# Binarised convolutions and a spline: mask rows interleaved by channel, the step chain on GpSimd, one load moved ahead of one store

## What is computed

```
out = relu(batchnorm(conv3x3(x, sign(w1))))       # gamma1, beta1; mean and variance over images and pixels
out = batchnorm(conv3x3(out, sign(w2)))           # gamma2, beta2
x   = relu(out + x)

u = (clip(x * a + b, -1.5, 1.5) + 1) * 0.5 * 31   # per channel a, b
i = floor(u);  t = u - i                          # cubic B-spline with 32 knots
spline = sum over n of alpha_table[clip(i + n - 1, 0, 31)] * basis_n(t)     # n = 0..3, 8 values each
y = id_gain * x + sum over r of spline[r] * mix[channel, r] + bias
```

## Time and profile before

| | us |
|---|---|
| median of 3 runs | 1140.85 |
| lowest, highest | 1138.58, 1143.94 |
| the profiled execution, as timed | 1139.08 |
| its span, from the first to the last instruction | 1137.2 |
| PE busy in it | 1081.0 (95%) |
| DVE busy | 966.2 (85%) |
| ACT busy | 899.3 (79%) |
| POOL busy | 137.5 (12%) |

### The profile page before, as it was taken

The page is one execution under the profiler, slowest core; times in us unless marked ns, Lnnn a source line. Parts: engine busy times, 40 slices in busy tenths (PEclk is TensorE's granted clock), DMA queues, the critical chain, the costliest instruction groups (busy, mean ns, idle before and its releaser), DMA issues.

```text
span 1137.2 us, 53175 instructions
## 1 busy us (share of the span) xinstructions
PE 1081.0 (95%) x24650; PEld 724.2 (64%) x24650; DVE 966.2 (85%) x959; ACT 899.3 (79%) x410; POOL 137.5 (12%) x195
## 2 busy tenths in 40 slices
PE   6999999699999968999999999999999999999996
PEld 5777777577777745556656656656666556656564
DVE  5856656687767779999999999999999998999997
ACT  4445443767777648999999999999999999999971
POOL 6000000058100000101101011011110110101100
PEclk9999999899999989999999999999999999999999
DMA  8677674677677936799898989989989988998652
GB/s 288 221 293 285 251 278 175 224 248 298 263 284 291 349 164 161 185 233 225 228 234 213 237 203 234 222 220 235 228 209 235 226 225 212 233 233 200 165 131 87
DMA packets 57465, 259.46 MB, mean 228 GB/s; under 512 B 16080, under 2 KB 16080, under 8 KB 49232
## 3 DMA queue, kind: packets, MB, share of 16 engines
q1 hardware_dynamic: 48496, 208.40, 54.6%
q0 software_dynamic: 8640, 48.17, 23.2%
q10 hardware_dynamic: 160, 0.30, 0.1%
HBM read 104.29 MB, written 77.07 MB: 159 GB/s over the span
## 4 chain that ended last, share of the span: by engine, by line
PE 86%; DVE 7%; issue 3%; DMA 1%; ACT 1%; SPq 0%; DVEq 0%; ACTq 0%
PE tab L1303 49%; PE acc L741 30%; PE tab L1313 7%; DVE middle_mask L1161 1%; DMA halo<-y_scratch 1%; DVE far_sq L1210 1%; DMA w_raw<-in_w 1%; ACT xin L381 1%; ACT yout L420 1%; DVE poly L1202 0%; DVE far L1188 0%; DVE stats L547 0%; DVE offset L1154 0%; DVE poly L1216 0%; DVE band_split L509 0%
## 5 line engine op out<-in xcount | busy, mean ns | idle before, releaser
L1303 PE MATMUL tab<-edge_mask,diag 128*32 128x392 bf16 x10240 | 446.6, 329 | 5.8 <-issue 2.5
L1303 PEld LDWEIGHTS tab<-edge_mask,diag 128*32 128x32 f16 x10240 | 283.5, 97 | 160.6 <-issue 20.1
L1058 ACT ACTIVATE edge_mask<-cell,thr 128x6272 bf16<-128x6272 bf16 x62 | 338.6, 5509 | 2.0 <-DMA cell<-cell 2.0
L420 ACT ACTIVATE yout<-acc 128x1568 f32<-128x1568 f32 x64 | 94.5, 1477 | 167.5 <-PE acc L741 146.9
L741 PE MATMUL acc<-band_split,w 64*64 64x385 f16 (+2 forms) x4608 | 194.6, 329 | 9.9 <-DVE band_split L509 4.9
L741 PE MATMUL acc<-split,w 64*64 64x385 f16 (+3 forms) x4608 | 191.5, 326 | 11.2 <-DVE w L468 10.0
L1303 PE MATMUL tab<-middle_mask,diag 128*32 128x392 bf16 x4096 | 187.2, 329 | 7.5 <-issue 5.5
L547 DVE BATCH_NORM_STATS2 stats<-yout 128x392 f32 (+1 forms) x240 | 117.9, 555 | 89.1 <-ACT yout L420 89.1
L741 PEld LDWEIGHTS acc<-band_split,w 64*64 64x64 f16 x4608 | 150.0, 109 | 54.3 <-issue 8.8
L741 PEld LDWEIGHTS acc<-split,w 64*64 64x64 f16 x4608 | 144.7, 108 | 57.1 <-issue 11.9
L1303 PEld LDWEIGHTS tab<-middle_mask,diag 128*32 128x32 f16 x4096 | 110.6, 97 | 72.6 <-DVE middle_mask L1161 10.4
(11 more groups left out here) (140 smaller groups left out, 962.0 us busy)
## 6 DMA issues: line engine op xcount, KB each, us to landing
y_scratch<-yout SPq DMA_DIRECT2D x32, 1568.0 KB, 6.2
cell<-cell SPq DMA_DIRECT2D x496, 98.0 KB, 4.6
xin<-y_scratch SPq DMA_DIRECT2D x16, 1568.0 KB, 6.2
lin<-far POOLq DMA_DIRECT2D x32, 784.0 KB, 8.6
out<-lin SPq DMA_DIRECT2D x31, 784.0 KB, 5.3
xin<-in_x SPq DMA_DIRECT2D x15, 1568.0 KB, 6.5
lin<-y_scratch SPq DMA_DIRECT2D x30, 784.0 KB, 9.3
lin<-in_x POOLq DMA_DIRECT2D x28, 784.0 KB, 7.9
```

Source lines behind the costliest of these rows:

```text
L420: act.activation(yout[b][:, :].rearrange("p (r k x) -> p k r x", r=2, k=TILES)[:, 2 * part:2 * part + 2], acc[:, 4 * part:4 * part + 4, 0: ...
L1058: act.activation(mask_of(c, q)[:, :, :], cell4[c % 2][:, :, :], ACT.Sign, bias=thr[:, q:q + 1]).then_inc(sign_mask_ready, 1)
L1303: mm = pe.matmul(tab[(c + t) % 2][j * GROUP:(j + 1) * GROUP, sub, 0:SUB], keep["diag"][part][:, j % 2, t, q, :], mask_of(c, q)[:, j, sub * ...
```

## The change

- **Mask rows.** Channel k of a block now stands on rows 4 k + g instead of 32 g + k. The 16 copies of a chunk write every fourth partition, `cell4[g:P:4]`, where they wrote 32 partitions in a row. `ident4`, `thr`, `above` and `mix_by_group` follow this order. GpSimd makes them with selects, a fold and 12 small arithmetic instructions instead of 32 memsets. `mix_by_group` is no longer loaded by 8 small DMAs but copied by 8 GpSimd instructions from `mix_sb`. `spread_cells` uses one matmul with 128 columns of weights where it used four with 32. Its weights lie in `dist_sq`, which for that is allocated for the whole kernel.
- **The steps' chain** moves from DVE to GpSimd, where it can run as soon as the coefficients are there, in the first convolution. With the new row order it takes 42 instructions. The last five instructions of `coefficients` no longer wait for each other.
- **SP's order.** At the end of the first convolution the load of pair 17 is issued before the store of pair 15, not after it.

The diff, cut to its core:

```diff
@@ -236,9 +241,6 @@
-                for g in range(4):
-                    sp.dma_start(mix_by_group[:, half, g * GROUP:(g + 1) * GROUP],
-                                 mix_t[:, half * GROUP:(half + 1) * GROUP]).then_inc(small_loaded, 16)
@@ -292,8 +294,8 @@
                         sp.wait_ge(stored[b], 16)
                         for to, frm in load(PAIRS + b, b, 1):
                             sp.dma_start(to, frm).then_inc(loaded[b], 16)
-                    if b == 0 and is_last(n):
-                        store(2 * i + 1, 1)
+                if is_last(n):
+                    store(2 * i + 1, 1)
@@ -309,6 +311,40 @@
+            def fold(t, width):
+                while width > 1:
+                    width //= 2
+                    link(pool.tensor_tensor(t[:, 0:width], t[:, 0:width], t[:, width:2 * width], ALU.add))
+            def steps():
+                for l in range(3):
+                    link(pool.tensor_tensor(step[:, l, :, :], coef[:, l, :, 1:CENTRES], coef[:, l, :, 0:STEPS],
+                                            ALU.subtract))
...
+                for half in range(2):
+                    for odd, quads in enumerate((EDGE_QUADS, MIDDLE_QUADS)):
+                        to = dsel[:, half, :, quads[0]:quads[1] + 1]
+                        for g in range(4):
+                            frm = step[:, 1 + half, :, 2 * g + odd:STEPS:8]
+                            if g == 0:
+                                link(pool.tensor_scalar(to, frm, of_group[:, g:g + 1], None, ALU.mult))
+                            else:
+                                link(pool.tensor_scalar(own_step[:, :, :], frm, of_group[:, g:g + 1], None, ALU.mult))
+                                link(pool.tensor_tensor(to, to, own_step[:, :, :], ALU.add))
...
@@ -319,19 +355,34 @@
+            link(pool.memset(keep["spread"][:, :, :], 0.0))
+            link(pool.affine_select(out=keep["spread"][:, :, :], in_=keep["spread"][:, :, :], compare_op=ALU.not_equal,
+                                    fill=1.0, base=0, pattern=[[-1, P], [0, 4]], channel_multiplier=1))
...
-                                        base=-g * GROUP, pattern=[[-1, GROUP]], channel_multiplier=1))
+                                        base=-g, pattern=[[-4, GROUP]], channel_multiplier=1))
...
+            pool.wait_ge(small_loaded, 5 * 16)
+            for half in range(2):
                 for g in range(4):
...
+                    pool.tensor_copy(mix_by_group[:, half, g:P:4],
+                                     mix_sb[:, half * GROUP:(half + 1) * GROUP]).then_inc(mix_spread, 1)
...
-            pool.wait_ge(steps_ready, 1)
+            pool.wait_ge(coefficients_ready, TABLES)
+            steps()
@@ -688,8 +719,6 @@
                     take_stats(2 * i, 0, base)
-                    if n == half_rounds:
-                        steps()
@@ -714,7 +743,8 @@
-                pe.wait_ge(small_loaded, 13 * 16)
+                pe.wait_ge(small_loaded, 5 * 16)
+                pe.wait_ge(mix_spread, 8)
@@ -935,7 +965,7 @@
-                        sp.dma_start(cell4[c % 2][g * GROUP:(g + 1) * GROUP, j, :],
+                        sp.dma_start(cell4[c % 2][g:P:4, j, :],
                                      cell[c % 2][j * GROUP:(j + 1) * GROUP, :]).then_inc(copied[c % 2], 16)
@@ -1320,13 +1350,11 @@
-                        for g in range(4):
-                            mm = pe.matmul(tab[s][g * GROUP:(g + 1) * GROUP, 2 * (j % 2) + u, 0:SUB],
-                                           ones[:, 2 * GROUP * j + 1:2 * GROUP * (j + 1):2],
-                                           cell[0][:, (2 * h + u) * SUB:(2 * h + u + 1) * SUB], start=True, stop=True)
+                        mm = pe.matmul(tab[s][:, 2 * (j % 2) + u, 0:SUB],
+                                       keep["spread"][:, j * GROUP:(j + 1) * GROUP, :],
+                                       cell[0][:, (2 * h + u) * SUB:(2 * h + u + 1) * SUB], start=True, stop=True)
```

68 lines of the change are left out of this document (38 added, 30 removed).

## The result

The changed kernel takes **1128.09 us** (median of 5, 1126.97 to 1131.77). The kernel before takes 1139.11 us (median of 5: the three runs that the prediction started from, and two more). The ratio is 0.990 [0.9874, 0.9925], so the gain is 11.0 us where 6.0 were forecast. The profiled execution took 1127.08 us, with a span of 1125.3. Its TensorE clock was 0.990 on average. In what follows "issue" is idle time of PE in which, by the profile, it waited for no other engine and no data.

A forecast was written before the change was run, and what follows sets the result against it. The prediction took PE, busy for 95% of the span, to bound the kernel. Terms of 2.5 (load), 2.0 (clock) and 1.5 us (second wait) made 6.0, so 1140.85 became 1134.8 us, range 1131 to 1139.

The forecast's parts named there:

- What bounds the kernel, and the start of pair 18: PE bounds the run; pair 18 in the second convolution starts at 236.5 instead of 242.47, 6.0 us sooner.
- Load ahead of the store: Pair 17's load, issued near 197, ends ACT's 2.47 us wait; PE starts pair 17 at 224.7, 2.5 us sooner.
- Clock: With pair 17's wait down to 0.85 us, PE's clock doesn't fall there, which gives 2.0 us.
- Not additive: Steps gone alone gain 1.5 us, the load alone 0 to 1.3 us, only both together 6.0 us.
- Steps on GpSimd and the opening: The chain on GpSimd is hidden and costs nothing; GpSimd's extra work at the start costs PE 0.2 us.
- The spread: In chunk 0's cells, 8 wide matmuls for 32 narrow ones gain 0.2 us, which cancels the opening's cost.
- The copies: In the spline, copies onto every fourth partition at 0.86 us an issue change nothing, since nobody waits for cheaper ones.
- Rival (c): Faster copies leave room for others, half of PE's 8.0 us of "issue" goes: 4.0 us more, 1130.8 us; chance 12%.
- The range: The whole kernel's time lies from 1131 to 1139 us, said to take in most of (c).

The follow-up runs named there:

- store_first: The changed kernel with pair 17's load issued behind the store of pair 15 again; 1131.8 us, ratio 0.9947 to the kernel before.
- load_alone: The kernel before with only pair 17's load moved ahead of the store of pair 15; 1139.9 us, ratio 1.0015 to the kernel before.
- steps_on_dve: The changed kernel with the steps' chain of 42 instructions back on DVE at its old place; 1137.5 us, ratio 0.9986 to the kernel before.
- read_strided: The kernel before, its copies writing 32 rows in a row but reading every fourth source row; 1137.0 us, ratio 0.9992 to the kernel before.

## Why the prediction was right and wrong

- **What bounds the kernel, and the start of pair 18**: right. The forecast was 236.5, and PE runs through it without a wait. Conv 2 is 5.8 us shorter between the two profiles, and 6.3 us by the means of all profiles (210.5 of seven with the old transition, 204.2 of ten with the new one). The forecast was 6.0.
- **Load ahead of the store**: right. It went out from 198.28 on (forecast near 197), ACT's 2.47 us are gone, and PE starts pair 17 at 225.42 - 210.45 = 14.97 us behind pair 16, where 224.7 - 209.63 = 15.07 was forecast.
- **Clock**: right, 1.00 in pair 17, behind a wait of 1.05 us (0.9 forecast). In store_first 2.67 us of standing still didn't lower it either; in load_alone 5.52 us did, and in steps_on_dve 9.70 us.
- **Not additive**: right for the load (nothing, and 5.52 us of wait instead), nearly right for the steps (2.2 by conv 2, 1.5 forecast).
- **Steps on GpSimd and the opening**: right, hidden. GpSimd gave way to DVE (3.42 us for one instruction), and DVE paid nothing that PE felt. In the first convolution the wait of 0.5 us for DVE's split at 50 us is even gone in the profiles of the changed kernel. The rule that whoever issues first holds the port pair (the Trainium skill, SBUF: State Buffer, Who interferes with whom) agrees with the row at 44.32, where DVE was first by 0.17 us. No pair of rows shown here has GpSimd first.
- **The spread**: 2.77 us for 8 wide matmuls against 2.80 for 32 narrow ones, where 0.2 was taken.
- **The copies**: this step failed. "Below, a cheaper copy gives nothing, since nobody waits" put the term at nothing, because it looked only at the engines that wait for the copies. The time to landing fell from 4.6 to 3.8 us, and beside the other edits 3.4 us came by the times, and 4.0 us by the splines of twelve profiles. Of these some 3 us are blocks of instructions that came late to PE, and they come by DMA too. Rival (c) named this very mechanism and gave 4.0 us for it at 12%. That its size came out was partly luck: that half of the "issue" would go was a guess, and the new rows alone gave only 0.5 us by the times. How the rows do it is shown in part. The packets of instructions took 1.04 to 1.12 us (medians over the spline) in the five profiles with the old rows and 0.96 in all seven with the new ones, but they start as late as with the old rows, 1.7 to 2.0 us after PE has begun the block before, against 1.8 to 1.9. The ports (the Trainium skill, SBUF: State Buffer, Door 1: The DMA port swizzle) would have the copies onto every fourth row land sooner, and they do. But read_strided, which spreads the source rows in the same way, landed later (4.9 us), so the ports aren't shown to be the cause.
- **The range** ended at 1131. The prediction says that it takes in "most of (c)", but (c)'s own figure, 1130.8, lies just outside it. The forecast started from a median of 1140.85, and the kernel before had medians of 1137.5 to 1139.1 later. That is 1.7 of the 6.7 us between 1134.8 and 1128.09. The forecast's 6.0 and (c)'s 4.0 make 10.0 us. The three ratios give 10.3, so the result of 11.0 us was also a little lucky.

What stays open: why the new rows alone, with the rest as before, gave only 0.5 us by the times; why half the copies gave nothing more in the changed kernel by the times; and what holds the packets of instructions back, above all beside large paced copies. No experiment here varied the instruction traffic itself.

## What to carry to other kernels

A transfer that nobody waits for is not free when the instructions of the engine that sets the end come by DMA too: look at where its "issue" gaps stand, count the instructions between them, set them beside the packets of its instruction queue, and see which burst of data comes just ahead. Look for several waits at one hand-over before pricing one of them; here two edits were worth 0 and 2 us apart and 6 together. And take a second profile of the same kernel before explaining a difference of a few us between two.

## What the runs showed of the hardware

- PE's instructions come in blocks of 256 (128 matmuls with their loads, 16.4 KB a packet), and a late block cost 0.15 to 3.8 us. PE went on 1.2 to 1.7 us after the block's packet had ended, in 208 of 213 cases. In all 3 to 9 us of a spline of some 705 us were lost so with 16 copies a chunk, 33 us with four copies of 392 KB, 52 us with these issued two by two.
- The same bytes in 4 broadcast copies instead of 16 took half the time to issue (6 to 7 us a chunk), landed in 7.4 us instead of 3.8, and made the kernel 2.9% slower than the changed one (1160.6 against 1128.1).
- A GpSimd instruction on 128 x 80 values that started 0.17 us behind a DVE instruction of 3.41 us took 3.42 us instead of 0.32.
- The granted clock fell to 0.50 behind waits of PE of 3.37, 5.52 and 9.70 us, and stayed at 1.00 behind waits of 1.05, 1.50 and 2.67 us.
- Copies onto every fourth row land in 3.8 us, onto 32 rows in a row in 4.6, four in a row onto the same 32 rows in 5.1, from every fourth row in 4.9.
